# A step-by-step recurrence on one Trainium2 core: three gates' split bf16 products replaced by float32 products, and the update rewritten over a common denominator

## The chip, the core and the metric

The kernel runs on one core of one Trainium2 chip. The core has five engines with a queue of instructions each: PE (TensorE, the 128x128 array; its weight loads are listed as PEld), DVE (VectorE), ACT (ScalarE), POOL (GpSimd) and SP (SyncE, which here only issues DMAs). An engine works through its queue in order, and engines meet only at semaphores. The metric is the device time of one execution in microseconds (us); lower is better.

## What is computed

The reference is a stack of layers: a transformer, a recurrence, the same transformer again, a mixture of experts, a full attention, and the experts again. The change touches the recurrence alone. Its input is x of shape (2, 1024, 128): B = 2 sequences, T = 1024 steps, 128 features. For each step, in order:

```
i_t = sigmoid(xi_t + h @ Wih)
f_t = sigmoid(xf_t + h @ Wfh)
g_t = tanh(xg_t + h @ Wgh)
o_t = sigmoid(xo_t + h @ Woh)
c_t = f_t * c + i_t * g_t
n_t = f_t * n + i_t * exp(g_t @ Weg + beg)
h_t = o_t * (c_t / n_t)
```

xi, xf, xg and xo are x times the upper halves of the weights plus a bias, and need no h. All is float32. Every step needs the h of the step before, so the 1024 steps are one chain.

## The kernel before, in words

The features lie on the 128 partitions, the two sequences side by side: a state or a gate of one step is a tile of 128x2. The function `recurrence_phase` does the recurrence. Its 1024 steps are 8 passes of a loop on the chip (`Fori`) of ROUND = 128 steps written out, and each round is 8 chunks of CH = 16 steps. Between rounds every semaphore of the phase is cleared and all engines meet at a barrier.

**Array.** The parts that need no h are computed a chunk ahead, by `project` (L1028): for each gate a product of the bias with ones, and one of the weights with 16 columns of x of each sequence, are put into a PSUM bank as the start of a sum (nine products in a chunk: the gate e, which is g_t @ Weg + beg, has a bias only). One is issued after every second step and one more after the first of a chunk. A step then adds its product with h to its two columns of the bank. For g this is one float32 product with h (L1048), for e one float32 product with tg, the tanh (L1060). For i, f and o, weight and h are each split into three bf16 parts, and six of the nine products of parts are added up (`recur`, L1032): 12 for i and f together, into the bank s, and 6 for o. The weights are split once, ahead of the loop, by four operations of DVE (L1004 to L1010). h is split in every step.

**ACT** (L1090 to L1099) does in every step tanh for tg, exp(-x) of i and f in one (es), exp(-x) of o (eo), and exp of e (ex), in this order.

**DVE** adds one to es (sg, L1110) and to eo (so, L1112), inverts sg (L1114), and works out, with so as a factor, n_t/o_t (no, L1127), c_t (cn, L1131), 1/no (L1133) and h (L1136). After that it splits h into three bf16 parts (hparts, L1138 to L1143) and last makes n_t (cn, L1146). That is 19 instructions a step. A value that a later instruction of the same engine reads is waited for with a semaphore, since the engine starts the next instruction before the one before has ended.

Some of these waits stand two in front of one instruction. At L1110 the instruction has the wait for n_done of the step before (written at the end of the loop's body) and the wait for es_ready in front of it; in the first step of a round it has the one for es_ready alone.

**POOL** adds h and x of a chunk of 16 steps into xB (L1156), off the chain.

Of the kernel before, what the change touches and what calls it, by code (L numbers as in the profile page):

```python
# [933 lines left out]
GATES = ("i", "f", "o", "g")  # L941

EARLY_TERMS = [(0, 0), (1, 0), (2, 0), (0, 1), (1, 1)]
LAST_TERM = (0, 2)

MOST = 1e37


def recurrence_phase(nc, c):

    with ExitStack() as ctx:
        sb, ps, sem = scope(nc, ctx)  # L960
        Wg = sb("Wgates", [P, 4, 2, P])
        Wparts = sb("Wparts", [P, 3, 3, P], BF16)
        wrest = sb("wrest", [P, 3, P])
# [8 lines left out]
        g_bank = [ps(f"g_bank{i}", [P, 512]) for i in range(2)]
        s_bank = [ps(f"s_bank{i}", [P, 512]) for i in range(2)]
        o_bank = [ps(f"o_bank{i}", [P, 512]) for i in range(2)]
        e_bank = [ps(f"e_bank{i}", [P, 512]) for i in range(2)]
        w_in, zeroed, w_split, table_loaded = sem("r_w_in"), sem("r_zeroed"), sem("r_w_split"), sem("r_table_loaded")
        counted = [sem("r_" + x) for x in (
            "g_done", "s_done", "o_done", "e_done", "tg_ready", "es_ready", "ex_ready", "eo_ready", "h_ready",
            "h_first", "h_split", "rest_done", "so_done", "nso_done", "sg_done", "fno_done", "ig_done", "n_done", "no_done", "rn_done", "y_done")]
        (g_done, s_done, o_done, e_done, tg_ready, es_ready, ex_ready, eo_ready, h_ready,  # L980
         h_first, h_split, rest_done, so_done, nso_done, sg_done, fno_done, ig_done, n_done, no_done, rn_done, y_done) = counted

        with nc.Block() as block:
# [9 lines left out]
            @block.gpsimd  # L993
            def _(pool):
                pool.memset(cn[:, :, :], 0.0).then_inc(zeroed, 1)
                pool.memset(hbuf[1][:, :, :], 0.0).then_inc(zeroed, 1)
                pool.memset(hparts[:, :, :], 0.0).then_inc(zeroed, 1)

            @block.vector
            def _(dve):  # L1000

                dve.wait_ge(w_in, 16 * 10)
                W = Wg[:, 0:3, 1, :]
                dve.tensor_copy(Wparts[:, :, 0, :], W).then_inc(w_split, 1)  # L1004
                dve.wait_ge(w_split, 1)
                dve.tensor_tensor(wrest[:, :, :], W, Wparts[:, :, 0, :], ALU.subtract).then_inc(w_split, 1)
                dve.wait_ge(w_split, 2)
                dve.tensor_copy(Wparts[:, :, 1, :], wrest[:, :, :]).then_inc(w_split, 1)
                dve.wait_ge(w_split, 3)
                dve.tensor_tensor(Wparts[:, :, 2, :], wrest[:, :, :], Wparts[:, :, 1, :], ALU.subtract).then_inc(w_split, 1)  # L1010

        def tensor_steps(pe, it, first_round):
            def project(j, at, which):


                gate, part = which // 2, which % 2
                if gate != 0 and gate != 1:
                    bank = {2: o_bank, 3: g_bank, 4: e_bank}[gate]
                    out = bank[j][:, 0:CH * B].rearrange("p (s b) -> p b s", b=B)
                    first = part == 0  # L1020
                else:
                    out = s_bank[j][:, 0:CH * 2 * B].rearrange("p (s g b) -> p g b s", g=2, b=B)[:, gate]
                    first = which == 0
                if part == 0:
                    lhsT, rhs = bias[0:1, gate, :], c.ones[0:1, 0:B * CH].rearrange("p (b s) -> p b s", b=B)
                else:
                    lhsT, rhs = Wg[:, gate, 0, :], c.xA[:, :, bass.ds(at, CH)]
                return pe.matmul(out, lhsT, rhs, start=first, stop=False, skip_group_check=True)  # L1028

            def recur(out, gate, terms):  # L1030
                for w_part, h_part in terms:
                    last = pe.matmul(out, Wparts[:, gate, w_part, :], hparts[:, h_part, :], start=False,  # L1032
                                     stop=(w_part, h_part) == LAST_TERM, skip_group_check=True)
                return last

            if first_round:
                for which in range(9):
                    project(0, PAD, which)
                return
            for n in range(ROUND):  # L1040
                k, s = divmod(n, CH)
                j = k % 2
                h = hbuf[j][:, :, s - 1] if s else hbuf[1 - j][:, :, CH - 1]
                i_out, f_out = (s_bank[j][:, (s * 2 + gate) * B:(s * 2 + gate + 1) * B] for gate in range(2))
                o_out = o_bank[j][:, s * B:(s + 1) * B]
                if n:
                    pe.wait_ge(h_ready, n)
                pe.matmul(g_bank[j][:, s * B:(s + 1) * B], Wg[:, 3, 1, :], h, start=False, stop=True,  # L1048
                          skip_group_check=True).then_inc(g_done, 1)
                if n:  # L1050
                    pe.wait_ge(h_split, 2 * n - 1)
                recur(i_out, 0, EARLY_TERMS)
                recur(f_out, 1, EARLY_TERMS)
                if n:
# [23 lines left out]
        with nc.Fori(0, T // ROUND) as it:  # L1078
            with nc.Block() as block:
# [5 lines left out]
                def _(act):  # L1085
                    for n in range(ROUND):
                        k, s = divmod(n, CH)
                        j = k % 2
                        act.wait_ge(g_done, n + 1)
                        act.activation(tg[:, :], g_bank[j][:, s * B:(s + 1) * B], ACT.Tanh).then_inc(tg_ready, 1)  # L1090
                        act.wait_ge(s_done, n + 1)
                        act.activation(es[:, :, :].rearrange("p g b -> p (g b)"), s_bank[j][:, s * 2 * B:(s + 1) * 2 * B],  # L1092
                                       ACT.Exp, scale=-1.0).then_inc(es_ready, 1)
                        act.wait_ge(o_done, n + 1)
                        act.activation(eo[:, :], o_bank[j][:, s * B:(s + 1) * B], ACT.Exp, scale=-1.0).then_inc(eo_ready, 1)
                        if n:
                            act.wait_ge(n_done, n)
                        act.wait_ge(e_done, n + 1)
                        act.activation(ex[:, :], e_bank[j][:, s * B:(s + 1) * B], ACT.Exp).then_inc(ex_ready, 1)  # L1099

                @block.vector
                def _(dve):

                    for n in range(ROUND):
                        k, s = divmod(n, CH)
                        j = k % 2
                        if s == 0 and k >= 2:
                            dve.wait_ge(y_done, k - 1)
                        dve.wait_ge(es_ready, n + 1)
                        dve.tensor_scalar(sg[:, :, :], es[:, :, :], 1.0, None, ALU.add).then_inc(sg_done, 1)  # L1110
                        dve.wait_ge(eo_ready, n + 1)
                        dve.tensor_scalar(so[:, :], eo[:, :], MOST, 1.0, ALU.min, ALU.add).then_inc(so_done, 1)  # L1112
                        dve.wait_ge(sg_done, 2 * n + 1)
                        dve.reciprocal(sg[:, :, :], sg[:, :, :]).then_inc(sg_done, 1)  # L1114
                        dve.wait_ge(so_done, n + 1)
                        dve.tensor_tensor(nso[:, :], cn[:, 1, :], so[:, :], ALU.mult).then_inc(nso_done, 1)
                        dve.wait_ge(sg_done, 2 * n + 2)
                        dve.tensor_tensor(iso[:, :], sg[:, 0, :], so[:, :], ALU.mult)
                        dve.wait_ge(nso_done, n + 1)
# [499 lines left out]
```

## Time and profile before

| | |
|---|---|
| median of 3 runs | 7952.26 us (7947.48 to 7956.73) |
| profiled execution, span from first to last instruction | 7947.7 us |
| recurrence, from the first tanh to the last h | 2334.0 to 5189.0 us |
| instructions of DVE, of ACT in the recurrence | 19, 4 a step |
| granted TensorE clock, mean of the span | 0.795 |

The profile is that of one execution, as the hardware's profiler took it. A clock of 1.00 is 2.4 GHz and 0.50 is 1.2 GHz. In a timeline a row gives the start, the time from the first start to the last end of what it merges, the engine, the line of the kernel, the operation, what is written and read, its shape and how many there are. In square brackets stands how long the engine was idle just before, and who ended that. A float32 product is in the profile two weight loads (LDWEIGHTS) and two MATMULs.

### The profile page before, as it was taken

To read this page: it belongs to the slowest core of one execution; us is meant where nothing else is said; L and a number is where in the kernel's file an instruction comes from. 1 tells how busy PE (TensorE), PEld (TensorE's weight loads), DVE (VectorE), ACT (ScalarE), POOL (GpSimd) and SP (SyncE) were. 2 spreads that over 40 slices of the span, in tenths; PEclk is the share of its full clock that TensorE was granted. 3 is DMA by queue.
4 is the path that set the end of the run, shared out by engine and by line. 5 is a ranking of instruction groups with operands and counts; after the bars stand their busy time and mean duration, and the time that the engine had idled before them with its cause. 6 is when DMAs were issued, how large, how long until landed. Compare 5 with 4: busy or idle time off the path is not lost. (4 is left out here: it accounts for less than half of the span.)

```text
span 7947.7 us, 238408 instructions
## 1 busy us (share of the span) xinstructions
PE 6508.3 (82%) x89716; PEld 4710.8 (59%) x89716; DVE 5680.7 (71%) x26551; ACT 2813.2 (35%) x7328; POOL 1991.7 (25%) x2075
## 2 busy tenths in 40 slices
PE   8999999999976666666666666679999999999887
PEld 5656656565656565655656565656565655656544
DVE  6676767676767777777777777777666676767566
ACT  4444444444432222222222222234444444444311
POOL 4343535353510000000000000034444353535200
PEclk9999999999975555555555555589999999999898
DMA  0000000000000000000000000000000000000000
GB/s 28 11 4 14 1 14 1 14 1 14 1 15 2 2 2 2 2 2 2 2 2 2 2 2 2 2 4 0 15 11 4 11 4 14 1 14 1 18 2 12
DMA packets 30765, 50.49 MB, mean 6 GB/s; under 512 B 2032, under 2 KB 25291, under 8 KB 28235
## 3 DMA queue, kind: packets, MB, share of 16 engines
q1 hardware_dynamic: 29614, 40.54, 1.6%
q8 instruction: 425, 6.96, 0.4%
q14 instruction: 314, 2.56, 0.1%
q10 hardware_dynamic: 412, 0.42, 0.0%
HBM read 39.91 MB, written 1.05 MB: 5 GB/s over the span
## 5 line engine op out<-in xcount | busy, mean ns | idle before, releaser
L1048 PE MATMUL g_bank<-hbuf,Wgates 128*128 128x2 f32 x2048 | 600.9, 363 | 1024.2 <-DVE hbuf L1136 970.3
L1048 PEld LDWEIGHTS g_bank<-hbuf,Wgates 128*128 128x128 f32 x2048 | 513.0, 311 | 1140.0 <-DVE hbuf L1136 1085.3
L1090 ACT ACTIVATE tg<-g_bank 128x2 f32<-128x2 f32 x1024 | 176.1, 172 | 1690.9 <-PE g_bank L1048 1690.9
L1156 POOL TENSOR_TENSOR xB<-hbuf,xA 128x32 f32 x64 | 16.4, 256 | 2853.0 <-DVE hbuf L1136 2853.0
L371 POOL TENSOR_TENSOR t1b<-t1b,t2b 128x1024 f32<-128x1024 f32 x192 | 451.7, 2354 | 687.1 <-DVE t2b L523 687.1
L371 POOL TENSOR_TENSOR t1a<-t1a,t2a 128x1024 f32<-128x1024 f32 x192 | 451.7, 2354 | 684.7 <-DVE t2a L523 684.7
L1060 PE MATMUL e_bank<-tg,Weg 128*128 128x2 f32 x2048 | 579.4, 352 | 0.0
L1032 PEld LDWEIGHTS s_bank<-hparts,Wparts 128*128 128x128 bf16 x12288 | 571.0, 117 | 0.0
L1110 DVE TENSOR_SCALAR sg<-es 128x4 f32<-128x4 f32 x1024 | 174.4, 170 | 554.5 <-ACT es L1092 554.5
L1060 PEld LDWEIGHTS e_bank<-tg,Weg 128*128 128x128 f32 x2048 | 515.1, 312 | 0.0
L1032 PE MATMUL s_bank<-hparts,Wparts 128*128 128x2 bf16 x12288 | 469.6, 165 | 0.0
L555 DVE TENSOR_REDUCE ssqb<-sqb 128x16 f32<-128x1024 f32 x192 | 232.7, 1215 | 187.5 <-ACT sqb L634 187.5
L376 POOL TENSOR_TENSOR t1b<-t1b,rnormb 128x1024 f32<-128x1024 f32 x192 | 361.1, 1902 | 11.6 <-DVE rnormb L98 11.6
L376 POOL TENSOR_TENSOR t1a<-t1a,rnorma 128x1024 f32<-128x1024 f32 x192 | 361.0, 1901 | 11.6 <-DVE rnorma L98 11.6
L555 DVE TENSOR_REDUCE ssqa<-sqa 128x16 f32<-128x1024 f32 x192 | 232.5, 1215 | 182.3 <-ACT sqa L634 182.3
L1127 DVE SCALAR_TENSOR_TENSOR no<-ex,iso,fno 128x1 f32<-128x1 f32 x2048 | 352.0, 213 | 3.6 <-issue 1.7
L1146 DVE SCALAR_TENSOR_TENSOR cn<-ex,sg,fcn 128x1 f32<-128x1 f32 x2048 | 351.8, 214 | 0.0
L431 PEld LDWEIGHTS banksa<-KT,QTa 64*32 64x32 f32 x12288 | 292.1, 107 | 41.0 <-issue 41.0
L431 PEld LDWEIGHTS banksb<-KT,QTb 64*32 64x32 f32 x12288 | 292.1, 107 | 40.7 <-issue 40.7
L643 ACT COPY Vwb<-banksb 128x512 f32<-128x512 f32 x384 | 224.8, 586 | 256.5 <-PE banksb L475 256.1
L643 ACT COPY Vwa<-banksa 128x512 f32<-128x512 f32 x384 | 224.7, 586 | 255.9 <-PE banksa L475 255.5
L431 PE MATMUL banksa<-KT,QTa 64*32 64x64 f32 x12288 | 308.3, 218 | 0.0
(435 smaller groups left out, 16401.7 us busy)
## 6 DMA issues: line engine op xcount, KB each, us to landing
Wqkv<-in_L_ffn_Wqkv SPq DMA_DIRECT2D x13, 1536.0 KB, 6.5
Wo<-in_L_ffn_Wo SPq DMA_DIRECT2D x13, 512.0 KB, 7.6
W<-in_L_ffn_W SPq DMA_DIRECT2D x12, 341.0 KB
W<-in_L_ffn_W SPq DMA_DIRECT2D x12, 128.0 KB
xt<-in_L_attn_x SPq DMA_DIRECT2D x2, 512.0 KB
rope<-in_rope SPq DMA_DIRECT2D x1, 1024.0 KB, 7.5
out<-ot SPq DMA_DIRECT2D x4, 256.0 KB
W<-in_L_ffn_W SPq DMA_DIRECT2D x12, 42.5 KB
```

What stands on the lines that cost most here:

```text
L371: pool.tensor_tensor(t1[:, part], t1[:, part], t2[:, part], ALU.add).then_inc(s.rot_sum, 1)
L376: pool.tensor_tensor(qview(t1[:, part]), qview(t1[:, part]), c.rnorm[:, i * HEADS:(i + 1) * HEADS].unsqueeze(2).to_broadcast([P, HEADS, DH ...
L431: last = pe.matmul(sc[WIN * w:WIN * w + WIN, col:col + KEYS], c.QT[rows, pair, WIN * w:WIN * w + WIN], c.KT[b][rows, pair, WIN * w:WIN * w ...
L555: dve.tensor_reduce(c.ssq[:, i * HEADS:(i + 1) * HEADS], qview(sq[:, i * INNER:(i + 1) * INNER]), AX.X, ALU.add).then_inc(s.ssq_done, 1)
L643: act.copy(c.Vw[:, w, :], vo[:, bank * 512:(bank + 1) * 512]).then_inc(s.v_ready, 1)
L1032: last = pe.matmul(out, Wparts[:, gate, w_part, :], hparts[:, h_part, :], start=False, stop=(w_part, h_part) == LAST_TERM, skip_group_chec ...
L1048: pe.matmul(g_bank[j][:, s * B:(s + 1) * B], Wg[:, 3, 1, :], h, start=False, stop=True, skip_group_check=True).then_inc(g_done, 1)
L1060: pe.matmul(e_bank[j][:, s * B:(s + 1) * B], Weg[:, :], tg[:, :], start=False, stop=True, skip_group_check=True).then_inc(e_done, 1)
L1090: act.activation(tg[:, :], g_bank[j][:, s * B:(s + 1) * B], ACT.Tanh).then_inc(tg_ready, 1)
L1110: dve.tensor_scalar(sg[:, :, :], es[:, :, :], 1.0, None, ALU.add).then_inc(sg_done, 1)
L1127: last = dve.scalar_tensor_tensor(out=no[:, b:b + 1], in0=ex[:, b:b + 1], scalar=iso[:, b:b + 1], in1=fno[:, b:b + 1], op0=ALU.mult, op1=A ...
L1146: last = dve.scalar_tensor_tensor(out=cn[:, 1, b:b + 1], in0=ex[:, b:b + 1], scalar=sg[:, 0, b:b + 1], in1=fcn[:, 1, b:b + 1], op0=ALU.mul ...
```

## The change

- The splitting of the weights and of h into bf16 parts is gone, with the tiles for it, and all five gates are one float32 product each. The order on the array is i, g, f, then e (which waits for tg), then o. i and o share a PSUM bank, g and e another, f has its own.
- ACT does exp(-i), tanh(g), exp(-f), exp(e), exp(-o), five operations of 128x2, in this order.
- With w = (1 + exp(-f)) / (1 + exp(-i)), DVE works out C = c + w·g and N = n + w·exp(e), which are c_t and n_t times the common denominator 1 + exp(-f). h is C / (N·(1 + exp(-o))), and c_t and n_t are C and N over the denominator, made after h. It is 13 instructions a step.
- `project` takes its pieces from a list that begins with the gate e.
- `recurrence_phase` gets a parameter `warm`, the number of extra bf16 products in a step; the call is unchanged, so it is 0 and there are none.

```diff
-EARLY_TERMS = [(0, 0), (1, 0), (2, 0), (0, 1), (1, 1)]
-LAST_TERM = (0, 2)
-MOST = 1e37
-def recurrence_phase(nc, c):
+MOST = 1e30
+def recurrence_phase(nc, c, warm=0):
...
-            @block.vector
-            def _(dve):
-                dve.wait_ge(w_in, 16 * 10)
...
-                dve.tensor_tensor(Wparts[:, :, 2, :], wrest[:, :, :], Wparts[:, :, 1, :], ALU.subtract).then_inc(w_split, 1)
+        def columns(gate, j, s, width=1):
+            bank, at = {"i": (io_bank, 0), "o": (io_bank, 1), "g": (ge_bank, 0), "e": (ge_bank, 1), "f": (f_bank, 0)}[gate]
+            at = (at * CH + s) * B
+            return bank[j][:, at:at + width * B]
...
+            pieces = [("e", 4, 0), ("i", 0, 0), ("i", 0, 1), ("f", 1, 0), ("f", 1, 1), ("o", 2, 0), ("o", 2, 1), ("g", 3, 0), ("g", 3, 1)]
...
+            def recur(gate, row, j, s, h):
+                return pe.matmul(columns(gate, j, s), Wg[:, row, 1, :], h, start=False, stop=True, skip_group_check=True)
...
                 if n:
                     pe.wait_ge(h_ready, n)
...
-                recur(i_out, 0, EARLY_TERMS)
-                recur(f_out, 1, EARLY_TERMS)
-                if n:
-                    pe.wait_ge(h_split, 2 * n)
-                recur(i_out, 0, [LAST_TERM])
-                recur(f_out, 1, [LAST_TERM]).then_inc(s_done, 1)
-                recur(o_out, 2, EARLY_TERMS + [LAST_TERM]).then_inc(o_done, 1)
+                recur("i", 0, j, s, h).then_inc(i_done, 1)
+                recur("g", 3, j, s, h).then_inc(g_done, 1)
+                recur("f", 1, j, s, h).then_inc(f_done, 1)
                 pe.wait_ge(tg_ready, n + 1)
...
+                pe.matmul(columns("e", j, s), Weg[:, :], tg[:, :], start=False, stop=True, skip_group_check=True).then_inc(e_done, 1)
+                recur("o", 2, j, s, h).then_inc(o_done, 1)
+                if s == 0:
+                    project(1 - j, 0, 0)
                 if s % 2 == 1:
...
+                    project(1 - j, it * ROUND + (PAD + (k + 1) * CH), 1 + s // 2)
+                for _ in range(warm if s % 2 == 0 else max(warm - 1, 0)):
+                    pe.matmul(spare[:, :], c.identb[:, :], c.mask[:, :, :].rearrange("p t j -> p (t j)"), start=True, stop=True)
...
+                        act.wait_ge(i_done, n + 1)
+                        act.activation(ei[:, :], columns("i", j, s), ACT.Exp, scale=-1.0).then_inc(ei_ready, 1)
                         act.wait_ge(g_done, n + 1)
...
+                        act.activation(tg[:, :], columns("g", j, s), ACT.Tanh).then_inc(tg_ready, 1)
+                        act.wait_ge(f_done, n + 1)
+                        act.activation(ef[:, :], columns("f", j, s), ACT.Exp, scale=-1.0).then_inc(ef_ready, 1)
+                        act.wait_ge(e_done, n + 1)
+                        act.activation(ex[:, :], columns("e", j, s), ACT.Exp).then_inc(ex_ready, 1)
                         act.wait_ge(o_done, n + 1)
...
+                        act.activation(eo[:, :], columns("o", j, s), ACT.Exp, scale=-1.0).then_inc(eo_ready, 1)
...
+                        dve.wait_ge(ei_ready, n + 1)
+                        dve.tensor_scalar(di[:, :], ei[:, :], 1.0, None, ALU.add).then_inc(di_done, 1)
+                        dve.wait_ge(di_done, n + 1)
+                        dve.reciprocal(ri[:, :], di[:, :]).then_inc(ri_done, 1)
+                        dve.wait_ge(ef_ready, n + 1)
+                        dve.tensor_scalar(df[:, :], ef[:, :], MOST, 1.0, ALU.min, ALU.add).then_inc(df_done, 1)
+                        dve.wait_ge(ri_done, n + 1)
+                        dve.wait_ge(df_done, n + 1)
+                        dve.tensor_tensor(w[:, :], df[:, :], ri[:, :], ALU.mult).then_inc(w_done, 1)
+                        dve.reciprocal(rf[:, :], df[:, :]).then_inc(rf_done, 1)
+                        dve.wait_ge(w_done, n + 1)
+                        for b in range(B):
+                            last = dve.scalar_tensor_tensor(out=up[:, 0, b:b + 1], in0=tg[:, b:b + 1], scalar=w[:, b:b + 1],
+                                                            in1=cn[:, 0, b:b + 1], op0=ALU.mult, op1=ALU.add)
+                        last.then_inc(c_done, 1)
+                        dve.wait_ge(ex_ready, n + 1)
+                        for b in range(B):
+                            last = dve.scalar_tensor_tensor(out=up[:, 1, b:b + 1], in0=ex[:, b:b + 1], scalar=w[:, b:b + 1],
+                                                            in1=cn[:, 1, b:b + 1], op0=ALU.mult, op1=ALU.add)
+                        last.then_inc(n_done, 1)
+                        dve.wait_ge(eo_ready, n + 1)
+                        dve.wait_ge(n_done, n + 1)
+                        dve.scalar_tensor_tensor(out=mo[:, :], in0=eo[:, :], scalar=1.0, in1=up[:, 1, :],
+                                                 op0=ALU.add, op1=ALU.mult).then_inc(mo_done, 1)
+                        dve.wait_ge(mo_done, n + 1)
+                        dve.reciprocal(rm[:, :], mo[:, :]).then_inc(rm_done, 1)
                         if s == 0 and k >= 2:
                             dve.wait_ge(y_done, k - 1)
...
+                        dve.wait_ge(c_done, n + 1)
+                        dve.wait_ge(rm_done, n + 1)
+                        dve.tensor_tensor(hbuf[j][:, :, s], up[:, 0, :], rm[:, :], ALU.mult).then_inc(h_ready, 1)
+                        dve.wait_ge(rf_done, n + 1)
+                        dve.tensor_tensor(cn[:, :, :], up[:, :, :], rf[:, :].unsqueeze(1).to_broadcast([P, 2, B]), ALU.mult).then_inc(state_done, 1)
+                        dve.wait_ge(state_done, n + 1)
```

## Rows read from the trace of the kernel before

**Rows 1.** Busy time by stretch: recurrence; first projections; weight split; a full-clock stretch.
```profile
core 0: us, PE busy (x) PEld busy (x) DVE busy (x) ACT busy (x) POOL busy (x), PEclk, DMA share, GB/s
2334.00:5189.00 2855.00, 1830.66 (x23677) 1709.63 (x23674) 2193.86 (x19451) 692.97 (x4096) 16.12 (x63) 0.50 0.01 2
...
2327.70:2332.90 5.20, 5.11 (x18) 4.48 (x18) 0.00 (x0) 1.49 (x2) 0.00 (x0) 0.50 0.00 0
...
2325.20:2327.70 2.50, 0.00 (x0) 0.00 (x0) 2.09 (x4) 0.00 (x0) 0.00 (x0) 0.50 0.00 0
...
2264.70:2266.70 2.00, 1.97 (x16) 1.86 (x16) 0.00 (x0) 1.23 (x2) 0.00 (x0) 1.00 0.00 0
```

**Rows 2.** One line, h of every step: durations, first and last start.
```profile
L1136 DVE TENSOR_TENSOR hbuf<-cn,rn x1024: 161/164/164, 2335.9 to 5188.9; 128x2 f32<-128x2 f32 x171
```

**Rows 3.** Waits of the recurrence: total, times, longest.
```profile
PEld g_bank L1048 <- issue: 54.1, 7, 8.2
```

**Rows 4.** Timeline of one step, h to h; the last row is two steps further on.
```profile
4002.45 0.16 DVE L1136 TENSOR_TENSOR hbuf<-cn,rn 128x2 f32<-128x2 f32 x1
...
4002.67 0.50 PEld L1048 LDWEIGHTS g_bank<-hbuf,Wgates 128*128 128x128 f32 x2 [1.32 <-DVE hbuf L1136]
4002.67 0.59 PE L1048 MATMUL g_bank<-hbuf,Wgates 128*128 128x2 f32 x2 [1.23 <-DVE hbuf L1136]
...
4003.30 0.17 ACT L1090 ACTIVATE tg<-g_bank 128x2 f32<-128x2 f32 x1 [1.59 <-PE g_bank L1048]
...
4003.57 0.50 PEld L1060 LDWEIGHTS e_bank<-tg,Weg 128*128 128x128 f32 x2
4003.60 0.57 PE L1060 MATMUL e_bank<-tg,Weg 128*128 128x2 f32 x2
4003.61 0.17 ACT L1092 ACTIVATE es<-s_bank 128x4 f32<-128x4 f32 x1
...
4003.89 0.17 DVE L1110 TENSOR_SCALAR sg<-es 128x4 f32<-128x4 f32 x1 [0.48 <-ACT es L1092]
4003.96 0.55 PEld L1028 LDWEIGHTS s_bank<-xA,Wgates 128*128 128x128 f32 x2
4003.98 0.17 DVE L1112 TENSOR_SCALAR so<-eo 128x2 f32<-128x2 f32 x1
4004.03 0.61 PE L1028 MATMUL s_bank<-xA,Wgates 128*128 x2
...
4004.19 0.15 DVE L1116 TENSOR_TENSOR nso<-cn,so 128x2 f32<-128x2 f32 x1
4004.26 0.17 ACT L1099 ACTIVATE ex<-e_bank 128x2 f32<-128x2 f32 x1 [0.32 <-PE e_bank L1060]
...
4004.53 0.15 DVE L1122 TENSOR_TENSOR ig<-sg,tg 128x2 f32<-128x2 f32 x1
4004.60 0.34 DVE L1127 SCALAR_TENSOR_TENSOR no<-ex,iso,fno 128x1 f32<-128x1 f32 x2
4004.86 0.15 DVE L1131 TENSOR_TENSOR cn<-ig,fcn 128x2 f32<-128x2 f32 x1
4004.98 0.17 DVE L1133 RECIPROCAL rn<-no 128x2 f32<-128x2 f32 x1
4005.18 0.16 DVE L1136 TENSOR_TENSOR hbuf<-cn,rn 128x2 f32<-128x2 f32 x1
...
4005.39 0.50 PEld L1048 LDWEIGHTS g_bank<-hbuf,Wgates 128*128 128x128 f32 x2 [0.89 <-DVE hbuf L1136]
...
4010.84 0.50 PEld L1048 LDWEIGHTS g_bank<-hbuf,Wgates 128*128 128x128 f32 x2 [0.80 <-DVE hbuf L1136]
```

**Rows 5.** Timeline, the same two operations in the first step of a round.
```profile
2334.32 0.17 ACT L1092 ACTIVATE es<-s_bank 128x4 f32<-128x4 f32 x1
...
2334.52 0.17 DVE L1110 TENSOR_SCALAR sg<-es 128x4 f32<-128x4 f32 x1 [7.07 <-ACT es L1092]
```

**Rows 6.** Timeline, sixteen float32 passes at the full clock.
```profile
2264.73 2.05 PE L459 MATMUL banksa<-OTa,Wo 128*128 128x128 f32 x16 [0.67 <-ACT OTa L623]
```

More of the change, by code:

```diff
@@ L972, in recurrence_phase @@
[L972 to L976, printed above, removed]
+        tg, ei, ef, eo, ex = sb("tg", [P, B]), sb("ei", [P, B]), sb("ef", [P, B]), sb("eo", [P, B]), sb("ex", [P, B])
+        di, ri, df, rf, w = sb("di", [P, B]), sb("ri", [P, B]), sb("df", [P, B]), sb("rf", [P, B]), sb("w", [P, B])
@@ L977, in recurrence_phase @@
+        cn, up = sb("cn", [P, 2, B]), sb("up", [P, 2, B])
+        mo, rm = sb("mo", [P, B]), sb("rm", [P, B])
+        io_bank = [ps(f"io_bank{i}", [P, 512]) for i in range(2)]
+        ge_bank = [ps(f"ge_bank{i}", [P, 512]) for i in range(2)]
+        f_bank = [ps(f"f_bank{i}", [P, 512]) for i in range(2)]
+        spare = ps("spare_bank", [P, 512])
+        w_in, zeroed, table_loaded = sem("r_w_in"), sem("r_zeroed"), sem("r_table_loaded")
         counted = [sem("r_" + x) for x in (
-            "g_done", "s_done", "o_done", "e_done", "tg_ready", "es_ready", "ex_ready", "eo_ready", "h_ready",
@@ L979, in recurrence_phase @@
[L979 to L981 removed]
+            "i_done", "g_done", "f_done", "e_done", "o_done", "ei_ready", "tg_ready", "ef_ready", "ex_ready", "eo_ready",
+            "h_ready", "di_done", "ri_done", "df_done", "w_done", "c_done", "n_done", "mo_done", "rm_done", "rf_done", "state_done", "y_done")]
@@ L983, in recurrence_phase @@
+        (i_done, g_done, f_done, e_done, o_done, ei_ready, tg_ready, ef_ready, ex_ready, eo_ready,
+         h_ready, di_done, ri_done, df_done, w_done, c_done, n_done, mo_done, rm_done, rf_done, state_done, y_done) = counted
         with nc.Block() as block:
@@ L1012, in tensor_steps @@
         def tensor_steps(pe, it, first_round):
+            pieces = [("e", 4, 0), ("i", 0, 0), ("i", 0, 1), ("f", 1, 0), ("f", 1, 1), ("o", 2, 0), ("o", 2, 1), ("g", 3, 0), ("g", 3, 1)]
             def project(j, at, which):
[L1016 to L1020, printed above, removed]
-                else:
-                    out = s_bank[j][:, 0:CH * 2 * B].rearrange("p (s g b) -> p g b s", g=2, b=B)[:, gate]
-                    first = which == 0
@@ L1024, in project @@
[L1024 to L1034, printed above, removed]
+                gate, row, part = pieces[which]
@@ new lines, in project @@
+                out = columns(gate, j, 0, CH).rearrange("p (s b) -> p b s", b=B)
+                if part == 0:
+                    lhsT, rhs = bias[0:1, row, :], c.ones[0:1, 0:B * CH].rearrange("p (b s) -> p b s", b=B)
+                else:
+                    lhsT, rhs = Wg[:, row, 0, :], c.xA[:, :, bass.ds(at, CH)]
+                return pe.matmul(out, lhsT, rhs, start=(gate in ("e", "i", "f") and part == 0), stop=False, skip_group_check=True)
+            def recur(gate, row, j, s, h):
+                return pe.matmul(columns(gate, j, s), Wg[:, row, 1, :], h, start=False, stop=True, skip_group_check=True)
@@ L1111, in _ @@
[L1111 to L1117, printed above, removed]
@@ L1125, in _ @@
-                        dve.wait_ge(ex_ready, n + 1)
-                        for b in range(B):
-                            last = dve.scalar_tensor_tensor(out=no[:, b:b + 1], in0=ex[:, b:b + 1], scalar=iso[:, b:b + 1],
-                                                            in1=fno[:, b:b + 1], op0=ALU.mult, op1=ALU.add)
-                        last.then_inc(no_done, 1)
-                        dve.wait_ge(ig_done, n + 1)
-                        dve.tensor_tensor(cn[:, 0, :], ig[:, :], fcn[:, 0, :], ALU.add)
@@ L1140, in _ @@
-                        dve.tensor_tensor(hparts[:, 1, :], h, hparts[:, 0, :], ALU.subtract).then_inc(h_split, 1)
-                        dve.tensor_tensor(hrest[:, :], h, hparts[:, 0, :], ALU.subtract).then_inc(rest_done, 1)
-                        dve.wait_ge(rest_done, n + 1)
-                        dve.tensor_tensor(hparts[:, 2, :], hrest[:, :], hparts[:, 1, :], ALU.subtract).then_inc(h_split, 1)
-                        for b in range(B):
-                            last = dve.scalar_tensor_tensor(out=cn[:, 1, b:b + 1], in0=ex[:, b:b + 1], scalar=sg[:, 0, b:b + 1],
-                                                            in1=fcn[:, 1, b:b + 1], op0=ALU.mult, op1=ALU.add)
@@ L1148, in _ @@
-                        last.then_inc(n_done, 1)
-                        dve.wait_ge(n_done, n + 1)
+                        dve.wait_ge(c_done, n + 1)
[3 more added lines that the diff above has]
+                        dve.tensor_tensor(cn[:, :, :], up[:, :, :], rf[:, :].unsqueeze(1).to_broadcast([P, 2, B]), ALU.mult).then_inc(state_done, 1)
```

50 lines of the change are left out of this document (removed).

## The prediction

> **What bounds the kernel now.** I read the stretches first. In the recurrence the array is busy 1831 of 2855 us and DVE 2194 of 2855 [rows 1]: neither is full, so a chain through several engines sets the pace. The line of h counts 1024 with first and last start 2853 us apart, 2.79 us a step [rows 2]; seven pauses between rounds are 54 us of that [rows 3]. Inside a round the step is (4010.84 - 4002.67)/3 = 2.72 us [rows 4]. That is the number the change must beat; a step saves or costs 1024 times.
>
> The chain inside a step [rows 4], from the first weight load at 4002.67 as zero: the g product ends at 0.59, tanh starts at 0.63, the e product at 0.90 and ex at 1.59. Beside it es starts at 0.94 and DVE takes it up at 1.22. From there DVE is back to back up to the pair at 1.93, though ex had ended at 1.76: the bound is DVE's chain behind i and f. After the pair come 1/no at 2.31, h at 2.51 and the next load at 2.72. The splitting of h and the last update run while the array works on g.
>
> The granted clock is 0.50 throughout the recurrence [rows 1], so every array time in rows 4 is one at 1.2 GHz.
>
> **The array's new part.** Removed: 18 bf16 products. Added: i, f and o as float32, five such products with g and e. What one costs behind another is seen where a projection follows e [rows 4]: first loads 0.39 apart, last loads' ends 0.44 (4004.07 to 4004.51), MATMUL ends 0.47 (4004.17 to 4004.64), the last with 32 columns instead of 2. I take 0.43. The low end is 0.39; the high end is the nine projections, busy 5.11 us [rows 1], 0.57 each. So i ends at 0.59, g at 1.02, f at 0.59 + 2 x 0.43 = 1.45.
>
> The Trainium skill (TensorE: Matmul & The Clock Gate, LDWEIGHTS) gives a load as its columns over 1.2 GHz, an estimated 0.107 us for 128. A float32 product of two such loads would follow another by 0.21, f would end at 1.02 and the time would be some 440 us lower than my sum. The trace disagrees: two loads of float32 take 0.44 here [rows 4], so the measured price stays.
>
> **ACT.** One instruction more. Product end to activation is 0.04, the activation 0.17 [rows 4]: exp(-f) runs from 1.49 to 1.66. exp(-i) and tanh run before it, on products 0.43 apart, so they hold nothing up.
>
> **DVE behind f**, the new path. From the end of an activation to DVE's start is 0.03 with one wait (2334.49 to 2334.52) [rows 5] and 0.11 with two (4003.78 to 4003.89) [rows 4]: at L1110 the wait that ends last is the second in the code. I price such a second wait at 0.08. It stands in the new code before w, before mo and before h, each time on a value of DVE itself. No row shows it for that case; it lies between 0 and 0.08, and I take 0.08, since the one row that shows a second wait ending last has that.
> - df: one wait, 1.66 + 0.03 = 1.69.
> - w: a dependent tensor_scalar costs 0.21 from start to start (so to nso [rows 4]); plus 0.08: 1.98.
> - the pair for C: a dependent operation, 0.20 as rn to h [rows 4]: 2.18. rf is issued in between, in the wait.
> - the pair for N: a pair occupies 0.26 (no to cn [rows 4]): 2.44.
> - mo: a pair whose end is waited for costs 0.38 (no to rn [rows 4]), plus 0.08: 2.90.
> - rm: mo is one operation with a constant, not a pointer: 0.20 as rn, up to 0.25 as the half of a pair and its end; I take 0.21 as the tensor_scalar, its nearest row: 3.11.
> - h: 0.20 + 0.08: 3.39.
> - next load: h to load 0.22 [rows 4]: **3.61**.
>
> In the old order the o term was already in n's factors when ex came: pair, 1/no, h. Here N's pair waits behind C's, the o term is multiplied in only after it (mo), and f, which starts the path, is the third product. Five of the six DVE instructions fewer come off behind h (six there before, L1138 to L1146, one now), which lay beside the array's work; they shorten nothing.
>
> **What is hidden, and by what.** di and ri: exp(-i) ends at 0.80, ri by 1.35, before w at 1.98. e: tanh runs 1.06 to 1.23, e is loaded 0.10 later at 1.33 (4003.47 to 4003.57) [rows 4], ex starts 0.69 after its load, at 2.02, and is with DVE at 2.22: 0.22 before N's pair. It would bind if e came that much later. o: e ends at 1.93, o at 2.36, eo at 2.57, with DVE at 2.60, against 2.90: 0.30 to spare. Behind eo on ACT waits only the next step's exp(-i), which needs h anyway. The projections come after o and end by about 3.0 of 3.6; without that cover they would cost 0.57 in nine of 16 steps, 0.3 a step. The state update after h takes DVE about 0.4 and the next ei arrives 0.80 after the load. PE's only waits are h, as before, and tg, before e: o is queued behind that wait and arrives in time all the same. POOL's addition and SP's DMAs are where they were; the wait for y_done moves from the top to h, once in a chunk, on the addition of the chunk before last.
>
> **Once.** The weights' split, 2.09 us of DVE with nothing beside it on the array [rows 1], goes: -2. Between rounds one more semaphore is cleared, and behind the last h DVE has one instruction left instead of six: 0 is taken, and 5 us either way in all. A pause is 7.7 us [rows 3], and nothing in the change bears on the rest of it.
>
> **The sum.** (3.61 - 2.72) x 1024 = +911, -2 = +909. The span of 7947.7 becomes about 8857. The median of the runs shown, 7952.3, is 4.6 above the profiled span, so the time predicted is **8861 us**, slower by 11%.
>
> **The rivals.**
>
> *The second waits are free* (20%). For it: a dependent operation with one wait costs only 0.03 to 0.04 over its duration [rows 4]; nothing shows that a wait on one's own engine pays like one on ACT. Against: rows 4 and 5, the same instruction with and without. Three times 0.08 less: step 3.37, (3.37 - 2.72) x 1024 - 2 = +664: 8616. The Trainium skill leans this way (VectorE: DVE Perf Modes, The DRAIN you can't avoid): a semaphore after each operation costs nothing extra, the number of operations is what counts. What speaks against that page here is that dependent operations start 0.20 apart, while ig and the pair behind it start 0.07 apart [rows 4].
>
> *The float32 products follow each other as slowly as the projections* (8%). Then 0.57 each, f at 1.73, everything behind it 0.28 later: step 3.89, (3.89 - 2.72) x 1024 - 2 = +1196: 9148. o would end at 2.87 and be with DVE at 3.11, still before mo at 3.18. Against it: the projections alternate between a bias of one partition and x, with 32 columns.
>
> *The clock rises to 2.4 GHz* (6%). The array will be busy 2.3 us of a step and 0.3 for projections, 73% against 64% now. At the full clock sixteen passes take 2.05 us at clock 1.00 [rows 1, 6], so 0.12 a pass and 0.24 a product; a lone product is 0.28 + 0.12 = 0.40, f ends at 0.88, and with the 2.16 behind it the step is 3.04: +328 - 2, 8278. Against it: during the nine projections the array was busy 5.11 of 5.20 us and the clock stayed at 0.50 [rows 1]. The Trainium skill has it otherwise (TensorE: Matmul & The Clock Gate, Part 1): a busy array releases the throttle. By that rule this rival would be the forecast; the row of the projections speaks against it, as far as one row can.
>
> *Not slower: the clock rises and DVE's chain is at its cheapest* (4%). The place is DVE behind f. The step is under 2.72 only if f's end and the 2.16 behind it are; at the full clock f ends at 0.88, so the chain must take 1.84 or less. Without the three second waits it is 1.92. With every dependent step at its cheapest (w, C's pair, rm, h: 0.06 less together) it is 1.86, and with 0.23 a product, since 2 columns may take less than the 128 of rows 6, f ends at 0.86: step 2.72, 7952 - 2 = 7950, no change; faster with 0.22. It decides from 1.86 us behind f, and only at 2.4 GHz.
>
> That the change does not do what it says, by adding products to the array, can't be here: warm is 0 in the only call.
>
> **How the numbers follow.** The forecast has 62%. Its own range is 8770 to 8960: the second wait at 0.05 takes 92 off, mo to rm at 0.25 and each second wait at 0.10 put 102 on. With the rival of free waits (20%) the range is 8 in 10: low 8590, a little under its 8616 for shorter tails, high 8960. The slow products, the full clock and the not-slower case, 18% together, are left out. About 0.2%, 16 us, is what a measurement of this kernel can tell from no change. The last rival is 0.03 within it and 0.01 faster; all else is slower: 0.96.
>
> **What would show it.** In a step of the changed kernel: DVE idle up to exp(-f) and in small gaps before w, mo and h; a gap of 0.11 after the end of what w waits for, if the second wait costs what I say, 0.03 if not; i, g and f ends 0.43 apart; exp(e) over before the pair for N starts; the clock 0.50. The step from load to load should be 3.61. The forecast is wrong if the clock row says 1.00, if the pair for N starts behind ex and not behind C's pair, or if mo starts behind eo.

## The result and the profile after

| | before | changed |
|---|---|---|
| median | 7949.87 us (7947.15 to 7956.73, 4 runs) | 8795.99 us (8792.51 to 8798.33, 4 runs) |
| span of the profiled execution | 7947.7 us | 8793.7 us |
| step inside a round | 2.72 us | 3.555 us |
| h of the first step to h of the last | 2853.0 us | 3698.9 us |

The ratio is 1.1059, with a 95% interval of 1.1044 to 1.1075. The forecast was 8861 us in a range of 8590 to 8960.

First the place. The busy time by stretch of the changed kernel, as in [rows 1], and its line of h, as in [rows 2]:

```profile
core 0: us, PE busy (x) PEld busy (x) DVE busy (x) ACT busy (x) POOL busy (x), PEclk, DMA share, GB/s
2334.00:6032.00 3698.00, 2647.44 (x11379) 2526.77 (x11380) 1915.17 (x13287) 879.12 (x5112) 15.23 (x63) 0.50 0.00 1
```

```profile
L1087 DVE TENSOR_TENSOR hbuf<-up,rm x1024: 161/164/165, 2338.9 to 6037.8; 128x2 f32<-128x2 f32 x171
```

From the first h to the last there are 845.9 us more than before, and the medians differ by 846.1: all of it is in the recurrence. The clock is 0.50 there as it was. The array is busy 72% of the time (64% before), DVE 52% (77% before): DVE has less to do, and the kernel is slower.

The waits in the recurrence tell how: the engine and line that waited, for whom, the total in us, how often, and the longest.

```profile
DVE di L1058 <- ACT ei L1041: 959.2, 1019, 14.5
DVE df L1062 <- ACT ef L1045: 415.3, 1011, 0.5
```

DVE now waits twice in a step for ACT, 0.9 for exp(-i) and again 0.4 for exp(-f). From there to h it waits for no other engine, only for its own results. The timeline of one step, as [rows 4], the start of the i product at 4001.88 being zero; the last row is two steps on:

```profile
4001.88 0.59 PE L995 MATMUL io_bank<-hbuf,Wgates 128*128 128x2 f32 x2 [1.26 <-DVE hbuf L1087]
...
4002.33 0.57 PE L995 MATMUL ge_bank<-hbuf,Wgates 128*128 128x2 f32 x2
...
4002.76 0.57 PE L995 MATMUL f_bank<-hbuf,Wgates 128*128 128x2 f32 x2
...
4003.16 0.51 PEld L1011 LDWEIGHTS ge_bank<-tg,Weg 128*128 128x128 f32 x2
...
4003.36 0.17 ACT L1045 ACTIVATE ef<-f_bank 128x2 f32<-128x2 f32 x1 [0.26 <-PE f_bank L995]
...
4003.56 0.17 DVE L1062 TENSOR_SCALAR df<-ef 128x2 f32<-128x2 f32 x1 [0.41 <-ACT ef L1045]
...
4003.79 0.17 ACT L1047 ACTIVATE ex<-ge_bank 128x2 f32<-128x2 f32 x1 [0.25 <-PE ge_bank L1011]
4003.84 0.16 DVE L1065 TENSOR_TENSOR w<-df,ri 128x2 f32<-128x2 f32 x1
...
4004.03 0.35 DVE L1069 SCALAR_TENSOR_TENSOR up<-tg,w,cn 128x1 f32<-128x1 f32 x2
...
4004.21 0.17 ACT L1049 ACTIVATE eo<-io_bank 128x2 f32<-128x2 f32 x1 [0.26 <-PE io_bank L995]
4004.30 0.34 DVE L1074 SCALAR_TENSOR_TENSOR up<-ex,w,cn 128x1 f32<-128x1 f32 x2
4004.75 0.16 DVE L1079 SCALAR_TENSOR_TENSOR mo<-eo,up 128x2 f32<-128x2 f32 x1
4004.95 0.17 DVE L1082 RECIPROCAL rm<-mo 128x2 f32<-128x2 f32 x1
4005.22 0.16 DVE L1087 TENSOR_TENSOR hbuf<-up,rm 128x2 f32<-128x2 f32 x1
...
4008.99 0.29 PEld L995 LDWEIGHTS io_bank<-hbuf,Wgates 128*128 128x128 f32 x1 [1.35 <-DVE hbuf L1087]
```

Two steps take 4008.99 - 4001.88 = 7.11 us. Against the forecast:

| after the load | forecast | measured |
|---|---|---|
| f ends | 1.45 | 1.45 |
| df | 1.69 | 1.68 |
| w | 1.98 | 1.96 |
| pair for C | 2.18 | 2.15 |
| pair for N | 2.44 | 2.42 |
| mo | 2.90 | 2.87 |
| rm | 3.11 | 3.07 |
| h | 3.39 | 3.34 |
| next load | 3.61 | 3.555 |

Three gaps are longer than those behind a single wait (0.20 to 0.21 for one operation, 0.38 for a pair [rows 4]): df to w 0.28, N's pair to mo 0.45, rm to h 0.27. Each stands where an instruction has two waits in front of it. exp(e) ends at 2.08 and exp(-o) at 2.50; neither binds.

### The profile page after: what moved, and what is told of

It reads as the page before. It is cut to its first block and busy times, and to the rows that moved or that the text cites. A ratio compares the mean times of both kernels' runs of the same rounds, so it can differ in the third digit from the quotient of the medians.

```text
span 8793.7 us, 209747 instructions
## 1 busy us (share of the span) xinstructions
PE 7330.2 (83%) x77428; PEld 5532.5 (63%) x77428; DVE 5402.3 (61%) x20403; ACT 3001.4 (34%) x8352; POOL 1990.8 (23%) x2074
## 5 line engine op out<-in xcount | busy, mean ns | idle before, releaser
L995 PE MATMUL io_bank<-hbuf,Wgates 128*128 128x2 f32 x4096 | 1180.3, 358 | 1051.8 <-DVE hbuf L1087 1000.8
L995 PEld LDWEIGHTS io_bank<-hbuf,Wgates 128*128 128x128 f32 x4096 | 1073.0, 322 | 1167.4 <-DVE hbuf L1087 1115.6
L995 PE MATMUL ge_bank<-hbuf,Wgates 128*128 128x2 f32 x2048 | 579.4, 353 | 0.0
L1011 PE MATMUL ge_bank<-tg,Weg 128*128 128x2 f32 x2048 | 579.4, 353 | 0.0
L995 PE MATMUL f_bank<-hbuf,Wgates 128*128 128x2 f32 x2048 | 579.3, 353 | 0.0
L995 PEld LDWEIGHTS ge_bank<-hbuf,Wgates 128*128 128x128 f32 x2048 | 560.2, 333 | 0.0
L995 PEld LDWEIGHTS f_bank<-hbuf,Wgates 128*128 128x128 f32 x2048 | 559.7, 333 | 0.0
L1011 PEld LDWEIGHTS ge_bank<-tg,Weg 128*128 128x128 f32 x2048 | 517.9, 313 | 0.0
L1069 DVE SCALAR_TENSOR_TENSOR up<-tg,w,cn 128x1 f32<-128x1 f32 x2048 | 358.9, 216 | 1.8 <-issue 1.5
L1074 DVE SCALAR_TENSOR_TENSOR up<-ex,w,cn 128x1 f32<-128x1 f32 x2048 | 351.7, 213 | 0.0
```

Source lines behind the costliest of these rows:

```text
L995: return pe.matmul(columns(gate, j, s), Wg[:, row, 1, :], h, start=False, stop=True, skip_group_check=True)
L1011: pe.matmul(columns("e", j, s), Weg[:, :], tg[:, :], start=False, stop=True, skip_group_check=True).then_inc(e_done, 1)
L1069: last = dve.scalar_tensor_tensor(out=up[:, 0, b:b + 1], in0=tg[:, b:b + 1], scalar=w[:, b:b + 1], in1=cn[:, 0, b:b + 1], op0=ALU.mult, op ...
L1074: last = dve.scalar_tensor_tensor(out=up[:, 1, b:b + 1], in0=ex[:, b:b + 1], scalar=w[:, b:b + 1], in1=cn[:, 1, b:b + 1], op0=ALU.mult, op ...
```

## The experiments

The theory at this point: the path goes through f, the third float32 product, and then through DVE alone, with C's pair ahead of N's and three second waits at 0.07. The rivals were free waits, exp(e) as the next bound, and the clock. The runs up to e8 are single ones; all but e4 differ from the changed kernel by clearly more than the 0.2% that a time varies by (e5, the closest, by 0.5%).

### e1: the waits turned round

```diff
-dve.wait_ge(ri_done, n + 1)
 dve.wait_ge(df_done, n + 1)
+dve.wait_ge(ri_done, n + 1)
 dve.tensor_tensor(w[:, :], df[:, :], ri[:, :], ALU.mult)
```

Likewise n_done ahead of eo_ready at mo, and rm_done ahead of y_done and c_done at h.

> The changed kernel with the order of the waits turned round in front of w, mo and h, so that the wait that ends last stands first. Theory (a second wait that ends last costs 0.07 us): each of the three gaps of the changed kernel (df to w 0.28, N's pair to mo 0.45, rm to h 0.27) shrinks by 0.07, the step goes from 3.555 to about 3.34, the time from 8796 to about 8580. Rival (waits are free, the gaps are how long the operations take to be seen): no change, 8796.

Measured: 8563.35 us. Timeline of e1, with its load at 3999.88:

```profile
4001.56 0.17 DVE L1062 TENSOR_SCALAR df<-ef 128x2 f32<-128x2 f32 x1 [0.41 <-ACT ef L1045]
...
4001.76 0.16 DVE L1065 TENSOR_TENSOR w<-df,ri 128x2 f32<-128x2 f32 x1
...
4002.22 0.34 DVE L1074 SCALAR_TENSOR_TENSOR up<-ex,w,cn 128x1 f32<-128x1 f32 x2
4002.60 0.16 DVE L1079 SCALAR_TENSOR_TENSOR mo<-eo,up 128x2 f32<-128x2 f32 x1
4002.80 0.17 DVE L1082 RECIPROCAL rm<-mo 128x2 f32<-128x2 f32 x1
4003.00 0.16 DVE L1087 TENSOR_TENSOR hbuf<-up,rm 128x2 f32<-128x2 f32 x1
...
4003.21 0.50 PEld L995 LDWEIGHTS io_bank<-hbuf,Wgates 128*128 128x128 f32 x2 [1.13 <-DVE hbuf L1087]
```

The gaps are 0.20, 0.38 and 0.20: each 0.07 to 0.08 shorter, by nothing but the order of the waits. The step is 3.33, and 233 us are gone. Free waits are refuted.

### e2: two second waits more

```diff
+dve.wait_ge(ef_ready, n + 1)
 dve.wait_ge(w_done, n + 1)
...
+dve.wait_ge(ex_ready, n + 1)
 dve.wait_ge(mo_done, n + 1)
```

> The changed kernel with one more wait, on a semaphore that has long been reached, put in front of the wait that binds, at C's pair (ef_ready) and at rm (ex_ready). Theory: both become second waits that end last, 0.07 each: step 3.555 to about 3.70, time about 8940. Rival (waits are free): 8796.

Measured: 8947.65 us, 152 more than the changed kernel, or 0.07 a step for each of the two. Timeline of e2, with its load at 4003.82:

```profile
4005.78 0.16 DVE L1065 TENSOR_TENSOR w<-df,ri 128x2 f32<-128x2 f32 x1
...
4006.05 0.35 DVE L1070 SCALAR_TENSOR_TENSOR up<-tg,w,cn 128x1 f32<-128x1 f32 x2
...
4006.77 0.16 DVE L1080 SCALAR_TENSOR_TENSOR mo<-eo,up 128x2 f32<-128x2 f32 x1
4007.03 0.17 DVE L1084 RECIPROCAL rm<-mo 128x2 f32<-128x2 f32 x1
```

w to C's pair is 0.27 instead of 0.19, and mo to rm 0.26 instead of 0.20. Taking the cost away and adding it give the same price.

### e3: N's pair ahead of C's

> The changed kernel with the pair for N in front of the pair for C; the wait for exp(e) moves ahead with it. Theory (e has 0.3 us to spare, the pair for C is 0.26 of the path): N's pair starts 2.15 after the load instead of 2.42, C's pair at 2.42, mo at 2.68 instead of 2.87, since it is queued behind C's pair: step about 3.36, time about 8600. Rival (exp(e) binds as soon as C's pair is out of the way): DVE waits for exp(e), less than half of that gain, above 8700.

Measured: 8626.77 us. Timeline of e3, load at 4001.66:

```profile
4003.84 0.35 DVE L1070 SCALAR_TENSOR_TENSOR up<-ex,w,cn 128x1 f32<-128x1 f32 x2
...
4004.11 0.34 DVE L1074 SCALAR_TENSOR_TENSOR up<-tg,w,cn 128x1 f32<-128x1 f32 x2
4004.37 0.15 DVE L1079 SCALAR_TENSOR_TENSOR mo<-eo,up 128x2 f32<-128x2 f32 x1
```

N's pair starts at 2.18, 0.24 earlier; mo at 2.71, behind C's pair. 169 us are gained: C's pair ahead of N's was on the path. The expectation was 0.03 low: exp(e) ended at 2.08 and is now the second wait of the pair and the last to end; the pair starts 0.10 behind it.

### e4 and e8: work for the array's idle time

```diff
-def recurrence_phase(nc, c, warm=0):
+def recurrence_phase(nc, c, warm=2):
```

and 4 in e8.

> The changed kernel with the parameter warm at 2: two products of 512 bf16 columns after the o product in even steps, one in odd ones, whose results nobody reads. Theory (what the array does in its idle time sets the clock; at 1.00 f ends at 0.88 instead of 1.45 and the chain behind it stays 2.10): granted clock 1.00 in the recurrence, step about 2.98, time about 8205. Rival (the clock stays at 0.50): the products fit in the array's idle time (o ends at 2.3, plus 0.86, against 3.55), no change, 8796.

> The changed kernel with warm at 4: four products of 512 columns in even steps, three in odd ones. With warm at 2 the array was busy 90% of the time and the clock stayed at 0.50. Theory (this clock does not follow the busy share that the profile shows; but more columns may raise it): if it rises to 1.00, a step of about 3.0 and about 8230; if it stays at 0.50, four products of 0.43 behind o at 2.3 end at 4.0 in even steps, and 0.57 + 3 x 0.43 behind it end at 4.2 in odd ones: step about 4.1 to 4.2, above 9300.

Measured: 8814.46 us with 2 and 9000.64 with 4. The busy time of a stretch inside the recurrence, e4 first, then e8 (columns as in [rows 1]):

```profile
4000.00:5000.00 1000.00, 899.46 (x3486) 699.44 (x3485) 518.15 (x3591) 237.56 (x1380) 4.12 (x17) 0.50 0.00 1
```

```profile
4000.00:5000.00 1000.00, 971.11 (x3774) 761.67 (x3841) 491.46 (x3417) 226.26 (x1314) 3.89 (x16) 0.50 0.00 1
```

The array is busy 90% and 97% of the stretch, and the clock is 0.50 in both, in the whole recurrence. So the full clock did not fail to come for want of busy time, as the profile counts it. That the Trainium skill (TensorE: Matmul & The Clock Gate, Part 1) has the clock released by a busy array is not borne out here. What would raise the clock in this phase stays open; no run here raised it. Of the 18 us that e4 takes more, 3 lie between its first and last h (3701.8 us against 3698.9).

In e8 the array was the bound, as assumed, but the expectation of over 9300 was too high. From the array's timeline:

```profile
4002.77 0.43 PE L995 MATMUL io_bank<-hbuf,Wgates 128*128 128x2 f32 x2
4003.05 0.57 PE L995 MATMUL ge_bank<-hbuf,Wgates 128*128 128x2 f32 x2
```

g starts 0.28 behind i, which follows the long products, and not 0.43 behind it; i's weight loads had begun at 4002.50, while the long products ran. Most steps take 3.65 to 3.68, where 4.0 and 4.2 were expected, so these 0.15 are less than half of the error. The rest is that whole durations were added up (0.57 for a projection, o's end at 2.30), where the projection of x and the product behind it start 0.43 apart.

### e5 and e6: the two halves of the change, alone

e5 is the kernel before with float32 products and its own update:

```diff
-recur(i_out, 0, EARLY_TERMS)
-recur(f_out, 1, EARLY_TERMS)
...
-recur(o_out, 2, EARLY_TERMS + [LAST_TERM]).then_inc(o_done, 1)
+recur(i_out, 0, h)
+recur(f_out, 1, h).then_inc(s_done, 1)
+recur(o_out, 2, h).then_inc(o_done, 1)
```

> The kernel before with i, f and o as one float32 product each and without the splitting of h; order g, i, f, o, e; its update is untouched. From the terms of the two traces: f ends at 1.45, exp of i and f is with DVE at 1.77, o ends at 1.88, so at 2.12, nso 2.33, fno 2.52, the pair at 2.74, rn 3.12, h 3.32, next load 3.53. Theory (the products alone cost 0.8 a step under the old update too): about 8780. Rival (the cost lies in the new update, the products are hidden as the old ones were): within 100 us of 7949.

> The kernel before with its bf16 products and its splitting of h, and the update of the changed kernel (one operation for 1 + exp of i and f, as before). From the terms: sum of es at 1.22, 1/(1+exp(-i)) 1.43, w 1.63, C's pair 1.82, N's pair 2.09, mo 2.54, rm 2.74, h 3.01, next load 3.22. Theory (the new update is longer by itself by 0.5, since C's pair stands ahead of N's, the o term comes last and two second waits bind): about 8460. Rival (the update over a common denominator, with fewer operations, is no longer than the old one): 7949 or less.

Measured: 8753.49 us (e5) and 8465.78 us (e6). Timeline of e5, with its load at 4000.81:

```profile
4002.91 0.17 DVE L1103 TENSOR_SCALAR so<-eo 128x2 f32<-128x2 f32 x1 [0.18 <-ACT eo L1086]
...
4003.53 0.34 DVE L1118 SCALAR_TENSOR_TENSOR no<-ex,iso,fno 128x1 f32<-128x1 f32 x2
...
4004.32 0.50 PEld L1045 LDWEIGHTS g_bank<-hbuf,Wgates 128*128 128x128 f32 x2 [1.31 <-DVE hbuf L1127]
```

so is at 2.10 where it was at 1.31 [rows 4], and everything behind it is as far apart as before: the products cost 0.79 a step. Of the kernel before, the bf16 products of i and f in the step of [rows 4]:

```profile
4003.12 0.46 PE L1032 MATMUL s_bank<-hparts,Wparts 128*128 128x2 bf16 x12
```

Twelve of them take 0.46 us and end at 0.91, while a single float32 product takes 0.43; in e5 i and f end at 1.43, and o, on which so waits, at 1.87 instead of 1.07. Timeline of e6, with its load at 4001.97:

```profile
4003.19 0.17 DVE L1106 TENSOR_SCALAR sg<-es 128x4 f32<-128x4 f32 x1 [0.67 <-ACT es L1092]
...
4005.19 0.50 PEld L1048 LDWEIGHTS g_bank<-hbuf,Wgates 128*128 128x128 f32 x2 [1.82 <-DVE hbuf L1133]
```

exp of i and f comes exactly when it did (sg at 1.22), and the step is 3.22: the new update costs 0.50 by itself. The two are not a sum. Products alone cost 804 us, the update alone 516, both 846. So neither half has a share of its own: the products cost 804 under the old update and 330 under the new one, the update 516 with the old products and 42 with the new ones. With float32 products the old update waits for the o term, which comes late, and the new one takes o last, so the one delay covers most of the other.

### e7: o ahead of e

> The changed kernel with the o product ahead of the e product, and exp(-o) ahead of exp(e) (o in a bank of its own). e ends at 2.30 instead of 1.86, exp(e) is with DVE at 2.54. Theory (e has 0.31 to spare before N's pair at 2.42): the pair moves by 0.12, step 3.67, about 8920. Rival (e is on the path already): the full 0.43, about 9240; rival (e is never on it): 8796.

Measured: 8919.66 us. Timeline of e7, with its load at 4003.05:

```profile
4005.38 0.17 ACT L1047 ACTIVATE ex<-ge_bank 128x2 f32<-128x2 f32 x1 [0.26 <-PE ge_bank L1012]
4005.59 0.35 DVE L1072 SCALAR_TENSOR_TENSOR up<-ex,w,cn 128x1 f32<-128x1 f32 x2
```

With e one product later, exp(e) starts at 2.33 instead of 1.91, and N's pair at 2.54 instead of 2.42: of the 0.42, 0.30 were spare. e was hidden in the changed kernel, by as much as its timeline shows.

### e9: DVE's costs so far taken off together

```diff
-for b in range(B):
-    last = dve.scalar_tensor_tensor(out=up[:, 0, b:b + 1], in0=tg[:, b:b + 1], scalar=w[:, b:b + 1],
...
 last.then_inc(n_done, 1)
+dve.tensor_tensor(up[:, 0, :], w[:, :], tg[:, :], ALU.mult).then_inc(c_done, 1)
...
+dve.wait_ge(c_done, 2 * n + 1)
+dve.tensor_tensor(up[:, 0, :], up[:, 0, :], cn[:, 0, :], ALU.add).then_inc(c_done, 1)
 dve.wait_ge(mo_done, n + 1)
```

> The changed kernel with all that the runs showed to lie on its path in DVE taken off: the waits turned round (e1), N's pair first (e3), and C by two tensor_tensor operations that start in the gaps, w*g behind N's pair and the sum with c behind mo. From the terms: w 1.88 after the load, N's pair 2.10, mo 2.48, rm 2.67, h 2.87, next load 3.08. Theory (what is left is the array: f ends at 1.45 and 1.6 lie behind it): time about 8310, so still some 4.5% behind the kernel before. Rival (something else, exp(e) above all, binds before that): 8400 or more.

Measured: 8462.16 us (8456.21 to 8471.26, 4 runs), ratio to the kernel before 1.0642 (1.0624 to 1.066). Timeline of e9, with its load at 4001.06:

```profile
4002.96 0.17 ACT L1047 ACTIVATE ex<-ge_bank 128x2 f32<-128x2 f32 x1 [0.25 <-PE ge_bank L1011]
...
4003.24 0.35 DVE L1070 SCALAR_TENSOR_TENSOR up<-ex,w,cn 128x1 f32<-128x1 f32 x2
4003.39 0.17 ACT L1049 ACTIVATE eo<-io_bank 128x2 f32<-128x2 f32 x1 [0.26 <-PE io_bank L995]
...
4003.67 0.16 DVE L1076 SCALAR_TENSOR_TENSOR mo<-eo,up 128x2 f32<-128x2 f32 x1
```

The rival was right. exp(e) ends at 4003.13 and the pair starts 0.11 later; exp(-o) ends at 4003.56 and mo starts 0.11 later. Both are the second wait in this order, and with the rest out of the way they are the ones that end last. The step is 3.22 instead of 3.08. The array's outputs bound it now, through ACT, and it is 6.4% behind the kernel before. But e9 did not take all of DVE's costs off: at N's pair and at mo the wait that ends last is again the second one. An estimate, from the 0.07 of e1, is that the other order there would give back up to 0.07 a step, some 70 us; that was not run, and it would still leave the kernel over 5% behind.

### e10 and e11: the same lesson in the kernel before

e10 turns round both double waits of the kernel before, e11 the one at L1110 alone:

```diff
+dve.wait_ge(es_ready, n + 1)
+if n:
+    dve.wait_ge(n_done, n)
 dve.tensor_scalar(sg[:, :, :], es[:, :, :], 1.0, None, ALU.add).then_inc(sg_done, 1)
```

In both, the wait for y_done moves from there to h.

> The kernel before with its two double waits turned round: at L1110 es_ready ahead of n_done, at L1127 ex_ready ahead of fno_done, and the wait for y_done moved behind rn_done. Theory (a second wait costs 0.07 only where it ends last on the path; before, sg comes earlier, but so waits for exp(-o), which ends at 1.27, and nso, fno and no hang on so): step at most 0.02 shorter, 7930 to 7950. Rival (the second wait at L1110 is on the path): 0.07 a step, about 7878.

> As e10, but with L1127 as in the kernel before (fno_done first, ex_ready second); turned round are only the waits at L1110. In e10 the pair at L1127 began at 1.97 after the load instead of 1.93, 0.07 after fno's result was there. Theory (e10 lost its 0.04 a step because fno_done, which ends last there, had become the second wait; and so waits for exp(-o), so an earlier sg gives nothing): step 2.72 and 2.71 at best, 7935 to 7950, no change against the kernel before. Rival (the loss of e10 came from L1110, or from the moved wait for y_done): 7985 again. Rival (sg is on the path): about 7880.

Measured: e10 7986.85 us, ratio 1.0046 (1.0029 to 1.0063); e11 7938.66 us (7936.16 to 7943.94, 11 runs), ratio 0.9984 (0.9975 to 0.9993). Timeline of e10, with its load at 4001.32, then of e11, with its load at 4000.20:

```profile
4002.47 0.17 DVE L1110 TENSOR_SCALAR sg<-es 128x4 f32<-128x4 f32 x1 [0.41 <-ACT es L1092]
4002.63 0.17 DVE L1112 TENSOR_SCALAR so<-eo 128x2 f32<-128x2 f32 x1
...
4003.03 0.16 DVE L1120 TENSOR_TENSOR fno<-nso,sg 128x2 f32<-128x2 f32 x1
...
4003.18 0.15 DVE L1122 TENSOR_TENSOR ig<-sg,tg 128x2 f32<-128x2 f32 x1
...
4003.29 0.35 DVE L1127 SCALAR_TENSOR_TENSOR no<-ex,iso,fno 128x1 f32<-128x1 f32 x2
```

```profile
4001.34 0.17 DVE L1110 TENSOR_SCALAR sg<-es 128x4 f32<-128x4 f32 x1 [0.41 <-ACT es L1092]
4001.50 0.17 DVE L1112 TENSOR_SCALAR so<-eo 128x2 f32<-128x2 f32 x1
...
4002.05 0.15 DVE L1122 TENSOR_TENSOR ig<-sg,tg 128x2 f32<-128x2 f32 x1
4002.12 0.35 DVE L1127 SCALAR_TENSOR_TENSOR no<-ex,iso,fno 128x1 f32<-128x1 f32 x2
```

sg comes 0.07 earlier in both (1.15 and 1.14 against 1.22), but so stays at 1.31 and 1.30, since it waits for exp(-o). e10 loses at the pair: ig to the pair is 0.11 instead of 0.07. exp(e) had ended 0.11 before; it is fno, done at 1.87, that ends last, and e10 had made it the second wait. I had turned the waits by the name of the slower engine and not by the trace. e11 leaves that order alone, is 12.7 us faster than the kernel before (0.16%, outside its interval), and so is the fastest of all that ran. That the order of the waits gives these 12.7 us is not shown. In the traces its recurrence is 17.6 us shorter. The median step from h to h is 2.721 against 2.727, which makes 6 us over all steps. Another 10 come from steps that are over 0.1 longer than the median, nearly all at the same places of every round: 56 of them before, 18 in e11. Their number differs from kernel to kernel (25 in e10), and what causes them is open.

## Why the prediction was right

**The side and the mechanism.** The forecast named DVE's chain behind exp(-f) as the new path, with f as the third product at 1.45. It ended at 1.45, and df, w, C, N, mo, rm and h follow in the order and at the distances of the table above.

**The size.** 8861 was forecast, 8796 measured: 65 us too much on a change of 846. The term that was mis-sized is the dependent step. It was rounded to 0.20 and 0.21 from [rows 4]; measured are 0.19 behind a tensor_tensor, 0.20 behind a tensor_scalar and behind mo, and 0.07 for a second wait instead of 0.08. That makes 0.055 a step, or 56 us. Some 7 more come from the step of before, which I took as 2.72 from three steps; over all steps its median is 2.727. The median of before, 2.4 lower in these runs, accounts for the rest. The small terms left at nothing nearly cancel: the pauses between rounds are 3 us shorter in all, and the 2 us of the weights' split are not seen, since the time outside the first and last h is 5094.7 us before and 5094.8 after.

**The unknown price.** Whether a wait on DVE's own result pays like one on ACT's was bounded by 0 and 0.08 and taken at 0.08. e1 and e2 show 0.07 each way. In e1, where the wait that ends last stands first, dependent operations are 0.03 to 0.04 apart from end to start; where it stands second, as in the changed kernel, 0.10 to 0.11. The rule of the Trainium skill (VectorE: DVE Perf Modes, The DRAIN you can't avoid), that a semaphore after each operation costs nothing extra, does not hold in this trace: an operation that waits for nothing starts 0.07 behind the one before (rf behind w), one with a single wait 0.19 to 0.21, one with a second that ends last 0.27 to 0.28. The other price, of float32 products, was 0.43 as taken. The 0.21 that the prediction works out from the Trainium skill (TensorE: Matmul & The Clock Gate, LDWEIGHTS) for two loads is half of that, so a recorded float32 load costs 0.215 here, twice the 0.107 of that estimate.

**What was hidden.** e had 0.30 to spare (e7) where 0.22 was forecast: its load came at 1.28 and not at 1.33, and ACT started exp(e) 0.63 after it and not 0.69. ACT had two waits in front of exp(e) before and has one now. In the runs exp(e) starts 0.09 to 0.10 behind the e product where there are two (before, e5) and 0.04 to 0.05 where there is one (changed, e6), so a second wait seems to cost ACT some 0.05 as well; no run changed that alone. o was hidden as forecast, exp(-o) ending at 2.50 against mo at 2.87. The projections cost nothing: the median step is 3.555 with one and without.

**The rivals.** Free waits: refuted by e1. Slow products: the products are 0.43 apart. The full clock: the row is 0.50, and e4 and e8 show that more busy time, as the profile counts it, does not raise it. The price of this rival stays untested, and its 0.28 of a lone product stands in no row. The not-slower case hung on that clock and fell with it.

**What the prediction did not say.** It added one chain and did not ask what each half would do alone. e5 and e6 show that either would be slower by itself, by 804 and by 516 us, and that together they cost 846, because most of the two delays overlap. It also named f's place as the third product as a reason, and no run moves f; that its place counts rests on the timeline, where df follows exp(-f) by 0.03.

## What to carry to other kernels

In a chain of tiny operations, count dependent steps and not instructions: the change took away six of 19 DVE instructions and replaced 18 bf16 products by three float32 ones, and lost 11%. Twelve bf16 products had taken the array 0.46 us, and one float32 product takes it 0.43; and the new update, with fewer instructions, has more of them behind one another on the path. Where an instruction needs two waits, read in the trace which of them ends last, and put that one first; each one wrongly placed on the path cost 0.07 us a step here. Two halves of a change on the same path should be run apart before either is blamed.

## What the hardware showed that was not expected

- On DVE a second wait costs 0.07 us if it ends last and nothing that the trace shows if it ended before: 233 us for three of them in e1, by line order alone. Why it does stays open.
- With the array busy 97% of a millisecond (e8), the granted clock stayed at 0.50; a stretch of the kernel before that is busy 98% stands at 1.00 [rows 1].
- Behind a long bf16 product a float32 one takes 0.28 instead of 0.43; its weight loads begin while the long one runs (e8).
- Twelve bf16 products of 2 columns take about as long on the array as one float32 product, 0.46 against 0.43 us, both at a clock of 0.50.
